# A new beginning for the attention and expert pipeline of one core: TensorE warmed, five places for x, weight halves moved to GpSimd, a shorter routing, gathers behind combinations

## The chip, the cores and the metric

The kernel runs on one core of a Trainium2 chip. The metric is the device time of one execution in microseconds (us). The engines are TensorE (PE, its weight loads PEld), VectorE (DVE), ScalarE (ACT) and GpSimd (POOL); SP, ACT and POOL issue DMAs.

## The reference

x is 8 batches of 512 tokens of 256 channels, in float32. One block is computed:

```python
xn = layernorm(x)
out = x + attn(xn) + ffn(xn)
# attn: latent = xn @ w_kv_down (256->128); k, v = latent @ w_kv_up; q = xn @ w_q
#       16 heads of 64, scores / 8, causal mask, softmax, y @ w_out
# ffn:  scores = sigmoid(xn @ gate_w.T + lb_bias); top 2 of 8 experts, weights normalised
#       for each expert e: wmean = mean weight of the tokens that chose e
#       out += where(chosen, mlp_e(xn) * wmean, 0);  mlp = silu(x gw) * (x uw) @ dw
#       out += shared mlp(xn)
```

The gate's results decide which tokens go to which expert, so they must be exact enough that no choice changes.

## The kernel before, in words

**Halves.** Most products are made from two rounded halves of each float32 operand, H and L = value − H, as three products HH, HL, LH (the helper `three`, lines 673 to 675). ACT copies H (`copy`, line 870), and a subtraction on DVE (`low`, line 1154) or on POOL makes L. Each weight passes through this once, in pieces `split_w` ("d", kA, qA, vA for the first two or four heads, and qB, kB, vB for the rest), `w_out`, and `split_moe` for the ten experts' weights, which are stored to HBM (`wm_scratch`) and loaded again for each block.

**Order.** `work_order` writes one list of ticks by hand. The 128 heads of all batches are taken in pairs P = 0 to 63. A pair lasts four units u, so u = 4P is its start; work with another rhythm is placed by `at(u, ...)`. In a pair: `recip`, `scores` of pair P+1 in three steps, what is placed at 4P, `attend` of pair P−1, `transposes` of the probabilities of the pair's two heads in three steps each, and what is placed at 4P+1 to 4P+3. What is placed before u = 0 is the prologue. Each engine walks the same ticks in order and does its share of a piece some ticks later (`LAG`). An engine never overtakes its own order: it waits at a semaphore with all that comes after.

**Pieces around the change.** `norm_stats` (DVE bn_stats and bn_aggr, then the reciprocal root on POOL), `norm_scale` (DVE, then a store of the normalised x), `norm_rows` (PE transposes to channels on partitions, ACT and DVE make the halves in `wr` or, for batch 0, `xs`), `gate_logits` and `gate_columns`. The seven later batches' transposed x is stored to `xs_scratch` and loaded again 32 units apart. x itself has two places in `acc`, so the load of batch b+2 waits until batch b is transposed and stored. `latent`, `query` and `key` make q and k of a pair (one place for each, `qk`, so their copies wait for the scores of the pair before), `value` makes v of half of four heads, `out_part` multiplies by w_out.

**Routing.** When all logits are there, `route_ops` finds the two experts of each token, counts them (two products by a matrix of ones and a triangle, `totals`), and works out the slot of each token in 39 blocks of 256: 64 DVE operations and four copies, each waiting for the one before. Then `select` and `tokens` (16 steps) invert the slots. From u = 54 the blocks' rows are gathered from `xn_scratch` (`block_load`, POOL), transposed (`block_rows`), multiplied (`gate_up`, `down`) and stored to `y_scratch`.

**The end.** After the last block, for each batch, `rows_load` gathers eight sets of expert rows on POOL, each into the place that a `combine` (DVE) of the batch before has read.

Weights in their raw form stand in buffers that later work uses: raw q in two of the four probability buffers `pp`, raw k in `acc`, raw v in `xr`.

Of the kernel before, what the change touches and what calls it, by code (L numbers as in the profile page):

```python
# [10 lines left out]
ALU = mybir.AluOpType  # L11
# [19 lines left out]
ROUTE_SUMS = 23  # L31
ROUTE_GAP = 12
ROUTE_OPS = 64
# [7 lines left out]
BUSY_HEADS = range(7, 22)  # L41
# [5 lines left out]
AT = {"query": (0.0, 0.9), "key": (2.3, 2.0), "value": (1.1, 2.1), "out_part": (3.2, 0.2), "stats": -3.7,  # L47
      "scale": -2.2, "rows": -1.6, "first": 54.0, "last": 176.0, "split": -1.3, "experts": 23.0, "shared0": 17.0,
# [20 lines left out]
def work_order():  # L69
# [60 lines left out]
    now, loads = 0, [17.5] * 3  # L130
    for start, group in plan:
# [22 lines left out]
        for k in range(k0, k0 + len(group)):  # L154
            loads[k % 3] = max(loads[k % 3], AT["experts"] + 18)
# [79 lines left out]
def attention_moe_kernel(nc, x, w_q, w_kvd, w_kvu, w_out, gate_w, lb_bias, w_moe, consts, out):  # L235
    ctx = ExitStack()
    with ctx:
# [31 lines left out]
        w_raw = sb("w_raw", [128, 2, 768])  # L269
        hh = sb("hh", [128, 3, 2, 512], F32R)  # L270
# [38 lines left out]
        d_xin = [new_sem(f"d_xin{i}") for i in range(2)]  # L309
# [3 lines left out]
        d_xn = [new_sem(f"d_xn{i}") for i in range(2)]  # L313
# [1175 lines left out]
```

## Time and profile before

| | |
|---|---|
| median of three runs | 995.25 us (992.63 to 995.55) |
| the profiled execution | 993.73 us, span 991.9 us |
| instructions | 20064 |
| DMA | 142.76 MB, mean 144 GB/s |
| VectorE, ScalarE, GpSimd busy | 693.2, 666.1, 353.0 us |

A busy share is an average over stages. In a kernel in which one engine does nearly all that can be done in most stages, the places where that engine is idle tell more: the windows give them by stretch, the waits name what ended them, and the timeline shows what stood in between. An instruction's idle time is named with the instruction that released it. The granted clock is TensorE's, as a share of 2.4 GHz.

### The profile page before, as it was taken

The page shows a single profiled execution, that of the slowest core. Times are in us where ns is not written, and L with a number is a line of the kernel's source. Part 1 is how long each engine was busy: PE and PEld are TensorE (multiplying, and loading weights), DVE is VectorE, ACT ScalarE, POOL GpSimd, SP SyncE. Part 2 cuts the span into 40 slices and gives each one's busy share as a digit, 9 for nine tenths or more (in the row PEclk, how much of TensorE's full clock was granted, in tenths as well). Part 3 has the DMA queues.
Part 4 walks back from the last instruction along what each step waited for, and adds up shares of the span by engine and source line. Part 5 has one row for each costly group of instructions (what it writes and reads, how often), then busy time and mean ns, then how long its engine had stood idle before and what let it go on. Part 6 is the DMA issues. An engine that isn't in the chain of part 4 may idle for free.

```text
span 991.9 us, 20064 instructions
## 1 busy us (share of the span) xinstructions
PE 942.5 (95%) x7008; PEld 748.6 (75%) x7008; DVE 693.2 (70%) x2000; ACT 666.1 (67%) x1930; POOL 353.0 (36%) x349
## 2 busy tenths in 40 slices
PE   5589998999999999999999999999999999999998
PEld 4456776678878888888888878888787677777776
DVE  5779599876666576665666666666666677788874
ACT  3756767776776667766677766767667665677662
POOL 0231113653332344333443324343222544444431
PEclk9799999999999999999999999999999999999999
DMA  7387424643326256453554444546434343433321
GB/s 226 125 318 259 163 74 146 207 145 114 110 84 213 69 157 188 143 154 125 159 163 164 151 131 153 163 140 165 149 127 150 93 126 115 150 107 108 107 76 43
DMA packets 66003, 142.76 MB, mean 144 GB/s; under 512 B 7856, under 2 KB 40880, under 8 KB 64112
## 3 DMA queue, kind: packets, MB, share of 16 engines
q1 hardware_dynamic: 52896, 91.77, 28.3%
q0 software_dynamic: 12432, 49.29, 15.8%
q8 instruction: 57, 0.93, 0.4%
q10 hardware_dynamic: 576, 0.42, 0.2%
q14 instruction: 42, 0.34, 0.1%
HBM read 104.76 MB, written 36.70 MB: 143 GB/s over the span
## 4 chain that ended last, share of the span: by engine, by line
PE 72%; DVE 13%; issue 9%; ACT 2%; another core or an unknown queue 2%; POOL 2%; DVEq 0%; POOLq 0%; ACTq 0%
PE PS L673 13%; PE PS L675 12%; PE PS L674 12%; PE PS L721 11%; PE PS L712 11%; PE PS L702 8%; DVE pp L1258 4%; PE PS L696 2%; PE PS L829 2%; DVE acc L1345 1%; DVE pt L1264 1%; DVE yf L1276 1%; DVE qk L1154 1%; DVE acc L1294 1%
## 5 line engine op out<-in xcount | busy, mean ns | idle before, releaser
L938 ACT ACTIVATE pp<-pp,nmax 128x128 f32<-128x128 f32 (+3 forms) x512 | 281.2, 553 | 110.4 <-DVE nmax L1258 76.0
L1258 DVE CUSTOM_DVE_ANT_0 pp<-PS,maskw 128x128 f32<-128x128 f32 (+3 forms) x512 | 216.7, 483 | 32.6 <-remote 23.8
L1419 POOL TENSOR_TENSOR yy<-yf,yy 128x512 fp32r<-128x512 f32 x63 | 81.5, 1293 | 260.2 <-ACT yy L870 259.8
L712 PE MATMUL PS<-ident,pp 128*128 128x128 f32 x1280 | 166.3, 276 | 1.4 <-ACT pt L870 0.6
L721 PE MATMUL PS<-pt,vv 128*64 128x512 f32 (+3 forms) x1024 | 154.5, 439 | 0.5 <-DVE nmax L1258 0.3
L712 PEld LDWEIGHTS PS<-ident,pp 128*128 128x128 f32 x1280 | 140.8, 140 | 17.7 <-issue 10.1
L721 PEld LDWEIGHTS PS<-pt,vv 128*64 128x64 f32 x1024 | 70.1, 136 | 91.4 <-issue 74.8
L702 PE MATMUL PS<-qk 64*128 64x256 f32 (+2 forms) x1152 | 122.2, 349 | 3.6 <-DVE acc L1294 2.2
L870 ACT ACTIVATE pt<-PS 128x384 f32<-128x384 f32 (+1 forms) x215 | 108.5, 512 | 4.1 <-PE PS L712 4.1
L1264 DVE COPY pt<-PS 128x384 f32<-128x384 f32 x169 | 99.2, 591 | 14.1 <-PE PS L712 12.0
L1413 POOL TENSOR_TENSOR hh<-hf,hh 128x256 fp32r<-128x256 f32 (+1 forms) x55 | 49.7, 903 | 138.3 <-ACT hh L870 136.7
L938 ACT ACTIVATION_READ_ACCUMULATOR pp<-pp,nmax 128x1 f32 x512 | 97.4, 190 | 0.0
L702 PEld LDWEIGHTS PS<-qk 64*128 64x128 f32 x1152 | 89.6, 188 | 9.4 <-issue 6.2
L1395 POOL DMA_INDIRECT xr<-xn_scratch,lg x78 | 74.5, 955 | 36.9 <-issue 13.8
L1406 POOL DMA_INDIRECT xg<-y_scratch,lg x64 | 63.3, 990 | 50.5 <-DVE acc L1345 35.4
L673 PE MATMUL PS<-woH,yy 128*128 128x256 f32 x256 | 78.1, 305 | 2.4 <-POOL yy L1419 2.0
L1240 DVE SCALAR_TENSOR_TENSOR qk<-PS,qk 128x512 fp32r<-128x512 f32 x64 | 44.0, 688 | 44.1 <-ACT qk L923 40.5
L674 PE MATMUL PS<-woL,yy 128*128 128x256 f32 x256 | 72.2, 282 | 0.0
L675 PE MATMUL PS<-woH,yy 128*128 128x256 f32 x256 | 72.2, 282 | 0.0
L870 ACT ACTIVATE yy<-yf 128x512 fp32r<-128x512 f32 (+1 forms) x65 | 40.4, 623 | 44.5 <-DVE yf L1276 38.2
L870 ACT ACTIVATE qk<-PS 128x128 f32<-128x128 f32 (+1 forms) x128 | 48.4, 429 | 24.8 <-PE PS L675 20.7
L1154 DVE TENSOR_TENSOR qk<-PS,qk 128x512 fp32r<-128x512 f32 x64 | 44.0, 688 | 28.8 <-ACT qk L870 28.6
(171 smaller groups left out, 2119.9 us busy)
## 6 DMA issues: line engine op xcount, KB each, us to landing
rb<-rr_scratch SPq DMA_DIRECT2D x128, 128.0 KB
wr<-wm_scratch SPq DMA_DIRECT2D x16, 768.0 KB, 5.7
y_scratch<-acc SPq DMA_DIRECT2D x39, 256.0 KB
acc<-in_x SPq DMA_DIRECT2D x15, 512.0 KB, 5.4
wm_scratch<-hh SPq DMA_DIRECT2D x10, 768.0 KB, 4.0
xs_scratch<-wr SPq DMA_DIRECT2D x7, 1024.0 KB, 5.7
xs<-xs_scratch SPq DMA_DIRECT2D x7, 1024.0 KB, 4.8
xn_scratch<-acc SPq DMA_DIRECT2D x8, 512.0 KB, 3.4
```

The lines of the kernel that those rows point to most:

```text
L673: e.matmul(o, aH, bH, start=first and i == 0, stop=False)
L674: e.matmul(o, aH, bL, start=False, stop=False)
L675: done = e.matmul(o, aL, bH, start=False, stop=last and i == len(pairs) - 1)
L702: done = e.matmul(bank(kind, i, 2 * j + h)[:, at:at + n], a[r, q], m[r, 0:n], start=first is True, stop=first is None)
L712: done = e.transpose(o, pp[:, i % 4, P_AT[t] + 128 * kt:P_AT[t] + 128 * kt + 128], ident[:, :])
L721: done = e.matmul(g[64 * h:64 * h + 64, 128 * kt:512], vv[:, i // 2 % 2, kt, n % 4, :], pt[:, h, PT_AT[kt]:PT_AT[kt] + 512 - 128 * kt], st ...
L870: return e.activation(o, i, ACT.Copy)
L938: e.activation(scores, scores, ACT.Exp, scale=-1.0, bias=nmax[:, b, t:t + 1], accum_out=rs[:, i % 4, 2 * t + h:2 * t + h + 1]).then_inc(a_ ...
L1258: e.tensor_tensor_reduce(pp[:, b, P_AT[t]:P_AT[t] + n], g[:, at:at + n], maskw[:, 512 - n:512], -1.0, 3e38, ALU.add, ALU.min, accum_out=nm ...
L1264: e.tensor_copy(pt_part(i, j), bank(kind, i, j)[:, 0:512 if j == 0 else 384]).then_inc(v_pt, 1)
L1395: e.indirect_dma_start(xr[:, 2 * (b % 2) + t, :], None, xn_d[:, :], bass.IndirectOffsetOnAxis(token_of[:, n:n + 1], 0)).then_inc(d_xr[b % ...
L1419: e.tensor_tensor(yy[:, i % 2, 1, :], yf[:, :], f32(yy[:, i % 2, 0, :]), ALU.subtract).then_inc(g_yl, 1)
```

## The change

- PE multiplies a constant by itself 15 times at the start and 5 times ahead of the first latent product (`warm`).
- The first batch's x comes by two queues. x has five places (two in `acc`, three in a new buffer `xp`); batches 1 to 4 are loaded at the start, 5 to 7 into places that come free. Seven batches are normalised 2.35 units apart instead of 2, somewhat later. The transposed x of the last batch goes to `xg`, the block buffer. ACT's queue issues the stores to `xs_scratch`.
- The halves L of qB, kB and vB are made on POOL. Query 1 and key 1 stand elsewhere in the prologue, and query 2 is ahead of scores 1. The mask is loaded as 128 columns, and POOL clears the rest.
- ACT makes all copies of transposed probabilities from head 2 to 21 (before: 7 to 21).
- Four experts are split ahead of the first shared block (before: two, in the prologue), the other six from u = 25.9.
- The routing has 51 operations, 38 of them ahead of the selection and 13 beside it; running sums are made by scan instructions, and the sums of weights by two products with 256 columns.
- At the end the gather for the next batch stands directly behind the combination that frees its place.

```diff
-ROUTE_SUMS = 23
+ROUTE_SUMS = 19
 ROUTE_GAP = 12
...
-BUSY_HEADS = range(7, 22)
+LATE_PARTS = WEIGHT_PARTS[4:]
+BUSY_HEADS = range(2, 22)
+EARLY_SPLITS = 4
...
+AT = {"query": (0.0, 0.9), "key": (2.3, 2.0), "value": (1.1, 2.1), "out_part": (3.2, 0.2), "stats": -1.6,
+      "scale": 0.2, "rows": 1.2, "first": 54.0, "last": 176.0, "experts": 25.9, "shared0": 19.2,
       "shared7": 248.0, "finish": (255.5, 257.2, 258.2), "fix": 8.0, "loading": 2.3, "xs": -9.4, "down": 4.6}
...
+    def norm_at(b):
+        return 2.35 * (b - 2) + 3.0 if b > 1 else 0.0
+
     for P in range(NHT // 2):
-        at(4 * (P - 2) + AT["query"][P % 2] if P else -9, "query", P)
-        at(4 * (P - 2) + AT["key"][P % 2] if P else -8, "key", P)
+        at(4 * (P - 2) + AT["query"][P % 2] if P > 2 else (-9, -6, -1.5)[P], "query", P)
+        at(4 * (P - 2) + AT["key"][P % 2] if P > 1 else (-8, -3.5)[P], "key", P)
     for Gr in range(NHT // 4):
         at(4 * (2 * Gr - 2) + AT["value"][0], "value", Gr, 0)
         at(4 * (2 * Gr - 1) + AT["value"][1], "value", Gr, 1)
...
             at(u + AT["xs"], "xs_load", b)
         at(u - 8.05 if b else -10, "latent", b)
         at(u + 8, "acc_load", b)
...
-        at(2 * b + AT["scale"], "norm_scale", b)
-        at(2 * b + AT["rows"], "norm_rows", b, 0)
-        at(2 * b + AT["rows"] + 0.05, "norm_rows", b, 1)
+        at(norm_at(b) + AT["stats"], "norm_stats", b)
+        at(norm_at(b) + AT["scale"], "norm_scale", b)
+        at(norm_at(b) + AT["rows"], "norm_rows", b, 0)
+        at(norm_at(b) + AT["rows"] + 0.05, "norm_rows", b, 1)
     for b in range(NBATCH):
-        at(2 * b + 0.7, "gate_logits", b)
-        at(2 * b + 1.8, "gate_columns", b)
+        at(norm_at(b) + 2.3 if b else 0.7, "gate_logits", b)
+        at(norm_at(b) + 3.4 if b else 1.8, "gate_columns", b)
     for c in range(2):
         at(4 * c, "w_out", c)
     for i in range(NW):
-        at(2 * i + AT["split"] if i < 2 else 2 * i - 4 + AT["experts"], "split_moe", i)
-    at(18, "routing")
+        at((8.0, 12.0, 15.0, 17.3)[i] if i < 4 else 2 * i - 8 + AT["experts"], "split_moe", i)
+    at(18.6, "routing")
     for i in range(3):
-        at(17.5, "ring_load", i)
...
         at(32 * b + 38, "store", b)
     for r, b in enumerate(FIX_ORDER):
         f = last_block + 8 + AT["fix"] * r
         for n in range(8):
-            at(f + 0.8 * n - (3 if r else 0), "rows_load", r, n)
+            if r == 0:
+                at(f + 0.8 * n, "rows_load", r, n)
             at(f + 3.3 + 0.65 * n, "combine", r, n)
+            if r + 1 < len(FIX_ORDER):
+                at(f + 3.31 + 0.65 * n, "rows_load", r + 1, n)
...
     for c in range(2):
         put("norm_rows", 0, c)
         tick()
+    put("split_w", "qA")
+    put("split_w", "vA")
 
...
         ticks[at_tick + int((k + ROUTE_GAP) * ROUTE_TICKS)].append(("route",))
-    end = at_tick + int((ROUTE_OPS + ROUTE_GAP) * ROUTE_TICKS)
+    end = at_tick + int((ROUTE_MAIN + ROUTE_GAP) * ROUTE_TICKS)
+    for k in range(ROUTE_OPS - ROUTE_MAIN):
+        ticks[end + 4 + 3 * k // 2].append(("route",))
...
+        def xT_flat(b):
+            return wr_flat(b % 2) if b < NBATCH - 1 else xg[:, :, :, :, :].rearrange("p q a c n -> p (q a c n)")
+
+        x_home = {b: (0, 1, 2, 3, 4, 0, 1, 2)[b] for b in range(NBATCH)}
+        x_turn = {b: sum(x_home[a] == x_home[b] for a in range(b + 1)) for b in range(NBATCH)}
+        x_next = {b: next((a for a in range(b + 1, NBATCH) if x_home[a] == x_home[b]), None) for b in range(NBATCH)}
+
         def x_in(b):
-            return acc[:, 1 + b % 2, :, :]
+            return acc[:, 1 + x_home[b], :, :] if x_home[b] < 2 else xp[:, x_home[b] - 2, :, :]
+
+        def x_stored(b):
+            return d_xn[x_home[b]], 16 * x_turn[b]
 
         def xT_part(b, c):
...
                 return xs[:, 0, c, :], xs[:, 1, c, :]
...
+                    e.dma_start(rows128(xn_d[i * T:i * T + T, :]), x_in(i)).then_inc(x_stored(i)[0], 16)
+                elif kind == "norm_rows" and lag == 4 and j and x_next[i]:
                     w.wait_ge(p_xt, 2 * i + 2)
-                    w.wait_ge(d_xn[i % 2], 16 * (i // 2 + 1))
-                    e.dma_start(x_in(i), rows128(x[i + 2])).then_inc(d_xin[i % 2], 16)
-                elif kind == "gate_logits" and lag == 0 and i >= 1:
-                    w.wait_ge(v_xtl, 2 * i + 2)
-                    e.dma_start(xs_d[i], f32(wr_flat(i % 2))).then_inc(d_xsd[i % 2], 16)
+                    w.wait_ge(*x_stored(i))
+                    e.dma_start(x_in(i), rows128(x[x_next[i]])).then_inc(x_loaded(x_next[i], 0)[0], 16)
                 elif kind == "xs_load" and lag == 0:
                     w.wait_ge(d_xsd[i % 2], 16 * ((i + 1) // 2) if i % 2 else 16 * (i // 2))
...
 
+            def warm(n):
+
+                for _ in range(n):
+                    e.matmul(bank("latent", 0, 0)[:, 0:128], ones[:, :], ones[:, :], start=True, stop=True)
+
+            w.wait_ge(g_cst, 1)
+            warm(15)
...
                     w.wait_ge(*xs_ready(b))
-                    w.wait_ge(v_wlo, whi_at["qA" if p < 2 else "qB"])
...
                 elif kind == "latent":
+                    if not i:
+                        warm(5)
...
-                    e.matmul(g2[:, 0:8], ones[:, :], e1[:, :], start=True, stop=True).then_inc(p_tot, 1)
+                    e.matmul(g2[:, 0:256], ones[:, :], rv("s"), start=True, stop=False)
+                    e.matmul(g2[:, 0:256], ones[:, :], rv("w"), start=False, stop=True).then_inc(p_tot, 1)
...
+            for t in range(2, 4):
+                e.dma_start(x_in(0)[:, t, :], x[0, 128 * t:128 * t + 128, :]).then_inc(d_x0[t], 16)
+            e.dma_start(ident[:, :], consts[:, 0:128]).then_inc(d_ident, 16)
             e.dma_start(gw[:, :, :], gate_w).then_inc(d_gw, 16)
-            e.dma_start(hf[:, 0, :], consts[:, 800:1312]).then_inc(d_mask, 16)
-            e.dma_start(lb[:, :], lb_bias).then_inc(d_lb, 16)
-            e.dma_start(kc[:, :], consts[:, 384:672]).then_inc(d_kc, 16)
 
...
                         w.wait_ge(d_wmd[s], 16 * (i // 2))
+                    if i >= EARLY_SPLITS:
...
+                elif kind == "gate_logits" and lag == 1 and i:
+                    w.wait_ge(v_xtl, 2 * i + 2)
+                    e.dma_start(xs_d[i], f32(xT_flat(i))).then_inc(d_xsd[i % 2], 16)
...
-                tt(rv(b_)[:, sh:256], rv(a_)[:, sh:256], rv(a_)[:, 0:256 - sh], ALU.add)
...
+            w.wait_ge(p_tot, 1)
+            w.wait_ge(g_cst, 1)
+            g, g2 = bank("totals", 0, 0), bank("totals", 1, 0)
+            own()
+            e.tensor_tensor_scan(rv("tot"), ones[:, 0:1].to_broadcast([128, 256]), g[:, 0:256], 0.0, ALU.mult,
+                                 ALU.add).then_inc(v_ro, 1)
+            yield
+            tt(rv("pos"), g[:, 256:512], rv("tot"), ALU.add)
+            yield
+            w.wait_ge(p_tot, 2)
+            reduce(wm[:, :], g2[:, 0:256].rearrange("p (t e) -> p e t", e=8), ALU.add)
+            yield
...
+            yield
+
+            cp(slot_of, m12[:, :])
+            yield
+            ts(e1[:, :], n_tok, 1.0, None, ALU.max)
+            yield
+            recip(e1[:, :])
+            yield
+            tt(wm[:, :], wm[:, :], e1[:, :], ALU.mult)
+            yield
+            for k in range(2):
+                tt(rv3("s"), rv3(f"c{k}"), bt(wm[:, :]), ALU.mult)
+                yield
+                reduce(coef[:, 32 * k:32 * k + 32], rv3("s"), ALU.add)
+                yield
...
+            e.memset(maskw[:, 0:384], 0.0).then_inc(g_cst, 1)
...
+                elif kind == "split_w" and lag == 0 and i in LATE_PARTS:
+                    raw, _, oH, oL = raw_w[i]
+                    w.wait_ge(a_whi, whi_at[i])
+                    e.tensor_tensor(oL, raw, f32(oH), ALU.subtract).then_inc(g_wlo, 1)
...
-                    e.tensor_tensor(out_w(i)[2], acc[:, 0, :, :].rearrange("p t n -> p (t n)"), f32(out_w(i)[1]),
-                                    ALU.subtract).then_inc(g_wo, 1)
+                    raw = acc[:, 0, :, :].rearrange("p t n -> p (t n)")
+                    for s in (slice(0, 512), slice(512, 1024)):
+                        done = e.tensor_tensor(out_w(i)[2][:, s], raw[:, s], f32(out_w(i)[1][:, s]), ALU.subtract)
+                    done.then_inc(g_wo, 1)
```

## Rows read from the trace of the kernel before

**Rows 1.** The page: busy time by engine, and PE's tenths in 40 slices.

```profile
PE 942.5 (95%) x7008; PEld 748.6 (75%) x7008; DVE 693.2 (70%) x2000; ACT 666.1 (67%) x1930; POOL 353.0 (36%) x349
...
PE   5589998999999999999999999999999999999998
```

**Rows 2.** Windows: busy of PE, PEld, DVE, ACT, POOL, then clock, DMA share, GB/s.

```profile
0.00:22.00 22.00, 10.42 (x51) 7.67 (x51) 9.99 (x31) 7.41 (x16) 1.85 (x8) 1.00 0.79 253
22.00:40.00 18.00, 7.66 (x42) 6.25 (x41) 14.80 (x43) 11.14 (x31) 3.32 (x3) 0.72 0.15 52
40.00:110.00 70.00, 63.16 (x436) 44.41 (x437) 54.26 (x176) 45.84 (x124) 17.93 (x18) 0.98 0.73 257
110.00:200.00 90.00, 82.56 (x608) 62.93 (x606) 79.20 (x228) 65.57 (x188) 32.21 (x26) 0.98 0.43 146
200.00:800.00 600.00, 596.43 (x4547) 486.17 (x4544) 390.52 (x1119) 415.37 (x1209) 225.42 (x228) 1.00 0.45 143
800.00:992.00 192.00, 182.23 (x1338) 141.14 (x1337) 144.40 (x406) 120.80 (x367) 72.25 (x67) 1.00 0.32 100
```

**Rows 3.** Waits of PE, 0 to 200 us: total, times, longest.

```profile
PE PS L696 <- DVE qk L1240: 13.8, 4, 10.3
PE PS L793 <- DVE acc L1175: 8.7, 1, 8.7
...
PE PS L673 <- DVE xs L1154: 1.4, 1, 1.4
PE PS L673 <- DVE wvL L1154: 1.2, 1, 1.2
```

**Rows 4.** Timeline, 0 to 40 us: start, length, instruction, idle before.

```profile
5.81 0.43 DVE L1164 BATCH_NORM_STATS2 st<-acc 128x6 f32<-128x256 f32 x1 [0.26 <-DMA acc<-in_x]
...
8.71 2.21 PE L793 MATMUL PS<-ident,acc 128*128 128x128 f32 x8 [8.71 <-DVE acc L1175]
...
12.92 0.63 PE L674 MATMUL PS<-xs,wdH 128*128 128x512 f32 x1
...
16.25 0.40 PE L674 MATMUL PS<-xs,wqH 128*128 128x512 f32 x1
...
20.32 1.82 PE L702 MATMUL PS<-qk 64*128 64x256 f32 x17
...
27.17 0.59 ACT L923 ACTIVATE qk<-PS 128x512 fp32r<-128x512 f32 x1
...
28.12 1.50 ACT L870 ACTIVATE wqH<-pp 128x1536 fp32r<-128x1536 f32 x1
...
29.65 1.76 DVE L1154 TENSOR_TENSOR wqL<-pp,wqH 128x1536 fp32r<-128x1536 f32 x1 [2.81 <-ACT wqH L870]
...
31.33 0.95 DVE L1154 TENSOR_TENSOR wkL<-acc,wkH 128x768 fp32r<-128x768 f32 x1
31.89 2.05 POOL L1371 TENSOR_TENSOR hh<-w_raw,hh 128x768 fp32r<-128x768 f32 x1 [3.60 <-ACT hh L870]
32.20 2.55 DVE L1154 TENSOR_TENSOR wvL<-xr,wvH 128x768 fp32r<-128x768 f32 x1
34.67 0.68 DVE L1240 SCALAR_TENSOR_TENSOR qk<-PS,qk 128x512 fp32r<-128x512 f32 x1
...
35.88 3.26 PE L702 MATMUL PS<-qk 64*128 64x256 f32 x18
```

**Rows 5.** Windows of 2 us, columns as in rows 2.

```profile
78.00:80.00 2.00, 2.00 (x9) 1.25 (x8) 2.00 (x8) 2.00 (x9) 0.00 (x0) 0.50 0.61 141
...
174.00:176.00 2.00, 2.00 (x6) 1.43 (x5) 2.00 (x8) 0.27 (x2) 0.88 (x2) 0.50 0.62 243
```

**Rows 6.** DVE's waits, 40 to 110 us; then the issues of one line.

```profile
DVE st L1164 <- DMA acc<-in_x: 3.8, 2, 3.0
```
```profile
L573 SPq DMA_DIRECT2D xs_scratch<-wr x7: 332/681/1753, 51.3 to 101.2; - x7
```

**Rows 7.** Waits of the whole run, POOL's for combinations.

```profile
POOL xg L1406 <- DVE acc L1345: 35.4, 13, 5.0
```

More of the change, by code:

```diff
@@ L129, in work_order @@
     plan.sort(key=lambda x: x[0])
-    now, loads = 0, [17.5] * 3
+    now, loads = 0, [17.0] * 3
     for start, group in plan:
@@ L308, in attention_moe_kernel @@
         d_x0 = [new_sem(f"d_x0{i}") for i in range(4)]
-        d_xin = [new_sem(f"d_xin{i}") for i in range(2)]
+        d_xin = [new_sem(f"d_xin{i}") for i in range(5)]
         d_ident, d_mask, d_gw, d_lb, d_kc = (new_sem("d_" + n) for n in ("ident", "mask", "gw", "lb", "kc"))
@@ L312, in attention_moe_kernel @@
         d_wout = new_sem("d_wout")
-        d_xn = [new_sem(f"d_xn{i}") for i in range(2)]
+        d_xn = [new_sem(f"d_xn{i}") for i in range(5)]
         d_xsd = [new_sem(f"d_xsd{i}") for i in range(2)]
@@ L373, in attention_moe_kernel, with low_weights @@
         whi_at = {n: i + 1 for i, n in enumerate(WEIGHT_PARTS)}
+        def low_weights(name):
+            return (g_wlo, whi_at[name] - 4) if name in LATE_PARTS else (v_wlo, whi_at[name])
         group_of = {k: item[-1] for k, item in enumerate(items)}
@@ L542, in hh_free @@
                 return ((p_dn, down_done(k - 3)),)
-            return tuple((sem, 16 if k < 2 else 16 * (NW // 2)) for sem in d_wmd)
+            return tuple((sem, 8 * EARLY_SPLITS if k < 2 else 16 * (NW // 2)) for sem in d_wmd)
         def f32(a):
@@ L549, in sync_program @@
             w = Waits(e)
-            for t in range(4):
+            for t in range(2):
                 e.dma_start(x_in(0)[:, t, :], x[0, 128 * t:128 * t + 128, :]).then_inc(d_x0[t], 16)
-            e.dma_start(ident[:, :], consts[:, 0:128]).then_inc(d_ident, 16)
             for name in WEIGHT_PARTS:
@@ L555, in sync_program @@
                 if name == "vA":
-                    e.dma_start(x_in(1), rows128(x[1])).then_inc(d_xin[1], 16)
+                    e.dma_start(hf[:, 0, 0:128], consts[:, 1184:1312]).then_inc(d_mask, 16)
+            for b in range(1, 5):
+                e.dma_start(x_in(b), rows128(x[b])).then_inc(x_loaded(b, 0)[0], 16)
+            e.dma_start(lb[:, :], lb_bias).then_inc(d_lb, 16)
+            e.dma_start(kc[:, :], consts[:, 384:672]).then_inc(d_kc, 16)
             def moe_load(q):
@@ L583, in sync_program @@
                     w.wait_ge(p_xt, 2 * NBATCH)
-                    for b in (NBATCH - 2, NBATCH - 1):
-                        w.wait_ge(d_xn[b % 2], 16 * (b // 2 + 1))
+                    for b in range(NBATCH - 3, NBATCH):
+                        w.wait_ge(*x_stored(b))
                     e.dma_start(rv("tri", 128), consts[:, 672:800]).then_inc(d_tri, 16)
@@ L900, in scalar_program @@
                     w.wait_ge(p_xt, 2 * NBATCH)
-                    for b in (NBATCH - 2, NBATCH - 1):
-                        w.wait_ge(d_xn[b % 2], 16 * (b // 2 + 1))
+                    for b in range(NBATCH - 3, NBATCH):
+                        w.wait_ge(*x_stored(b))
                     e.activation(rv("s"), lgf, ACT.Exp, scale=-1.0).then_inc(a_sig, 1)
@@ L1031, in route_ops @@
             w.wait_ge(p_xt, 2 * NBATCH)
-            for b in (NBATCH - 2, NBATCH - 1):
-                w.wait_ge(d_xn[b % 2], 16 * (b // 2 + 1))
+            for b in range(NBATCH - 3, NBATCH):
+                w.wait_ge(*x_stored(b))
             ts(rv("s"), rv("s"), 1.0, None, ALU.add)
```

147 lines of the change are left out of this document (60 added, 87 removed).

## The prediction

> **What bounds the kernel now.** The page comes first: TensorE (PE) is busy for 942.5 of 991.9 us, and its tenths are low only at the start [rows 1]. The windows then put the idle time in its place. From 200 to 800 us PE is idle 3.6 of 600 us: there the time is PE's own work, which the change leaves as it is, and every microsecond gained earlier is carried to the end one for one. Idle elsewhere: 11.6 us in 0 to 22, 10.3 in 22 to 40, 6.8 in 40 to 110, 7.4 in 110 to 200, 9.8 after 800 [rows 2]. So the most that a new beginning can give is some 36 us of idle and what the slow clock costs beside it. The waits name what ends the gaps: before 200 us nearly all are DVE's, one of 10.3 us, and 8.7 us are the wait for the first normalised x [rows 3].
>
> The 10.3 us gap can be read in the timeline. ACT is busy with exponentials until it copies key 1 at 27.17; then it rounds the late weights (28.12 on), DVE subtracts three of them in order (wqL, wkL, wvL, 29.65 to 34.75), and the low half of key 1 stands behind them and begins at 34.67. Scores 1 start at 35.4 [rows 4]. PE then comes back at about half pace: the 18 score matmuls take 3.26 us, where 17 took 1.82 before [rows 4]. In 78 to 80 and 174 to 176, each some us after a gap, the granted clock is 0.50, the level of 1.2 GHz [rows 5].
>
> The sum is made on the profiled execution: 993.73 us, with a span of 991.9 and 1.8 outside it. The median of the runs shown is 995.25, 1.5 above it.
>
> **To scores 0 (0 to 22 us).** Two of the four first x tiles move to ACT's queue, so the last is issued two slots of some 0.45 us sooner; bn_stats on it starts at 5.81 now [rows 4]. I take 1.1 us off the wait of 8.7. The 15 warming products run in that wait. The trace has no such product; the nearest row is the 8 transposes of 128 columns in 2.21 us, 0.28 each, so one instruction each gives 4.1 us and two each 8.3, begun at about 0.95: they end between 5.1 and 9.2, and x is due at about 7.6. Cost 0 to 1.6; I take 0, since the transposes of the row themselves wait for DVE. The gain is the clock: matmuls of 512 columns start 0.43 us apart from 12.33 to 15.5 and 0.23 apart after that (0.63 and 0.40 long [rows 4]); 7 at 0.2 are 1.4 us. The five further products stand in the 1.4 us wait for xs [rows 3] and are hidden. Splitting vA sooner removes a wait of 1.2 us, and query 1 now fills PE while key 0 is evicted. Idle goes from 11.6 to about 8.8: 2.8 + 1.4 = **4.2**, with scores 0 at about 17 in place of 20.1.
>
> **The late weights (22 to 40 us).** qB, kB and vB are subtracted on POOL. On DVE they took 1.76 + 0.95 + 2.55 = 5.3 us; POOL takes 2.05 us for 768 columns [rows 4], so 4.1 + 2.05 + 2.05 = 8.2 us. qB comes early: ACT rounds it right behind value 0 (1.50 us, to about 18), POOL is done at about 22. Query 2 needs it and is ahead of scores 1 in PE's order; its 1.4 us end at 23.4. Scores 1 need key 1: before, the copy was there 7.7 us after scores 0 had begun at 20.1, and its low half, 0.7 long, would have been at 8.4; the copy now comes after four exponentials instead of eight, so 6.5 to 8.4, that is 23.5 to 25.4. PE has about 5 us of work in between, which leaves a gap of 1.5 to 3.4; I take 2.8. What is late next is value (1,0), which needs vB. ACT copies query 2 only after scores 1, so it rounds kB and vB at about 26.3 to 27.8, and POOL is done 4.1 us later, about 31; PE gets there at about 28. I take 2.8 us (0 if vB's rounding slips ahead, 5 if POOL is held). Idle 10.3 becomes 5.6: 4.7, and the half clock behind it goes, 1.4 on the scores and 0.5 on their neighbours: **6.6**.
>
> POOL's row and DVE's give a ratio of 2.05 to 0.95, and wvL, which ran beside POOL's subtraction (31.89 to 33.94), took 2.55 us for the same 768 columns [rows 4]. The Trainium skill has both: GPSIMD Engine Reference, Engine selection, sends elementwise work with two inputs to VectorE, as GpSimd is about half as fast; SBUF — State Buffer, Who interferes with whom, says that a DVE instruction with two SBUF inputs and a GpSimd instruction that reads SBUF exclude each other for the whole instruction. The trace agrees with both. By these rules the move loses 3 us of engine time and could block DVE besides; what stands on DVE meanwhile are mostly reads of PSUM, which by the same section don't collide.
>
> **x in five places, norms further apart (40 to 110 us).** Now DVE waits 3.8 us for x [rows 6], and in this stretch it is busy 54.3 of 70 us in bursts [rows 2]. With four batches loaded at the start these waits go. The norms come every 2.35 units instead of 2, and all probability copies from head 2 on are ACT's. Per pair of heads that is, as an estimate from the durations in the timeline, about 13.7 us of DVE, 14 of ACT and 15.4 of PE, against 16.5 of DVE and 16.2 of PE before: PE becomes the bound, but narrowly. Idle 6.8 to 3.0: 3.8. Half clock at 77 to 80 gone: 1.3. **5.1**. The stores of xs move to ACT's queue. SP needs 0.33 to 1.75 us for an issue, median 0.68 [rows 6]: seven cost ACT 2.3 to 12.3 us, over 4.5 pairs. At the median that is 1.1 us per pair, just hidden; at the top ACT leads PE by some 1.5 us per pair, 7 us in all. Whether v_xtl is waited for costs nothing: ACT's copy of the logits ahead of it already stands behind it.
>
> **Routing (110 to 200 us).** DVE is busy 79.2 of 90 us [rows 2]. 64 operations and 4 copies become 51; 38 are ahead of the selection, 13 beside it. Some 17 fewer at 0.2 to 0.45 us are 5 to 6 us less of DVE. Of 7.4 us idle I leave 4.0, since the 13 now fall into the selection: 3.4. The slow clock at 171 to 176 [rows 5]: 1.4. The weight sums become two products of 256 columns instead of one of 8: 0.85 more PE. **3.95**. Four early expert splits move 1.8 us units of POOL and 0.8 of ACT forward into idle time.
>
> **The end.** Each gather stands right behind the combination that frees its place. POOL waits 35.4 us for those combinations now, to nobody's harm [rows 7]. 0 to 2 us, I take 0.5.
>
> Sum: 4.2 + 6.6 + 5.1 + 3.95 + 0.5 = 20.35; 0.6 is given back for a half clock after the two new gaps. 993.73 − 19.7 = **974.0 us**.
>
> **Rivals.** (A) As above, 974; its own range is 967 to 983. (B) The head is freed more fully: no gap for vB, no idle after 40 us. Then 4.2 + 11.2 + 8.1 + 8 + 2 = 33.5, and 960 to 967. For it speaks that PE reaches 10.0 of 10 wherever DVE isn't late; against it the narrow margins of 1.5 us per pair. (C) ACT or DVE becomes the bound in the first 20 units: the issues on ACT at 1.75 us (7 us lost), vB at 5 us, and routing's 13 late operations cost what they save (3.4): 974 + 7 + 2.2 + 3.4 = 986.6; 983 to 992. (D) On the other side, one mechanism at the end: POOL now stands at a gather until DVE has done the combination just ahead of it, and the low half of yy, which out_part waits for, stands behind on POOL. About 9 out_part groups lie in those 72 units. The slack is some 2 us; DVE is busy 144 of 192 us there [rows 2], and POOL's longest wait for a combination is 5.0 us [rows 7]. If each group costs more than 2.2 us, the 19.7 are gone; at 5.0 − 2.0 = 3.0 it is 27, so 1001. Against it: the wait exists already without PE waiting for POOL there. (E) The beginning gains but the gaps only move, within 0.3% (3 us, about what separates a real difference from none here): 992 to 997.
>
> **Numbers.** A 0.60, B 0.14, C 0.18, E 0.03, D 0.05. 966 to 987 keeps A nearly whole and the larger part of C, and leaves out about 2 in 10. Faster by over 0.3%: A, B and C, 0.92; same 0.03; slower 0.05.
>
> **What would show it.** Right: matmuls of the first latent 0.23 us apart; scores 0 near 17, scores 1 near 24, no PE gap over 4 us after 10 us; the idle sum before 200 us at 20 to 23 instead of 36.2; 200 to 800 unchanged. Wrong: a PE gap before query 2 or value (1,0) above 5 us (POOL too slow), xs stores of over 1 us on ACT with PE waiting for ACT between 40 and 90, new waits for POOL's yy after 760, or PE busy per window in the middle that differs.

## The result, and the profile after

The changed kernel takes 1013.06 us (median of 4 runs, 1011.01 to 1014.83); the kernel before, run beside it, takes 993.94 (4 runs, 991.66 to 995.55). The ratio is 1.0189, with a 95% interval of 1.0170 to 1.0208: slower by 1.9%, where 974.0 us and a range of 966 to 987 had been forecast. Case D, given 0.05 and 1001 us, is what happened, and it cost more than it was priced at. The profiled run took 1014.83 us, with a span of 1013.0. Of the executions of the experiments below, one of E6 (5102.92 us) and one of the kernel before (1530.11) were in a slow state, and the ratios leave them out.

The page after, as in [rows 1], with the tenths of the granted clock:

```profile
PE 955.4 (94%) x7050; PEld 762.3 (75%) x7050; DVE 675.2 (67%) x1973; ACT 670.7 (66%) x1937; POOL 361.5 (36%) x355
...
PE   8699998999999999999999999999997998888988
...
PEclk9999999999999999999999999999999898899999
```

PE's tenths fall towards the end, where [rows 1] has only nines up to the last, and the clock dips there too. The windows, columns as in [rows 2]:

```profile
0.00:22.00 22.00, 18.77 (x106) 15.31 (x106) 10.21 (x32) 9.62 (x19) 5.62 (x10) 1.00 0.82 258
22.00:40.00 18.00, 12.15 (x83) 8.34 (x82) 14.29 (x55) 15.85 (x48) 5.68 (x6) 1.00 0.34 107
40.00:110.00 70.00, 63.30 (x433) 44.76 (x432) 51.06 (x166) 50.38 (x138) 22.51 (x22) 0.95 0.74 260
110.00:200.00 90.00, 84.43 (x642) 64.80 (x641) 78.23 (x233) 63.85 (x183) 40.14 (x36) 1.00 0.50 169
200.00:800.00 600.00, 590.63 (x4487) 483.37 (x4487) 383.87 (x1095) 413.62 (x1202) 215.32 (x217) 0.99 0.44 138
800.00:1013.00 213.00, 186.15 (x1307) 145.68 (x1306) 137.51 (x394) 117.40 (x353) 72.22 (x67) 0.94 0.29 88
```

Against [rows 2], idle in 22 to 40 us falls from 10.3 to 5.9 and in 110 to 200 from 7.4 to 5.6; in 40 to 110 it stays (6.8 and 6.7) and the clock is lower (0.98 and 0.95). From 200 to 800 it goes from 3.6 to 9.4, and after 800 us from 9.8 to 26.9. The waits name the cause; first PE's, then POOL's, of the whole run (total, times, longest):

```profile
PE PS L700 <- POOL yy L1463: 29.5, 8, 7.0
```
```profile
POOL xg L1450 <- DVE acc L1382: 68.7, 24, 4.6
```

PE's wait for POOL's low half of yy, 2.0 us in 3 waits in the kernel before, is now PE's largest. Six of its 8 waits are long: 6.99 us at 786.55 (inside the window 200 to 800), and five of 4.25 to 4.35 after that. POOL's wait for combinations has doubled from 35.4 us in 13 to 68.7 in 24 [rows 7]. One such place, first on POOL and then on PE:

```profile
839.30 1.14 POOL L1450 DMA_INDIRECT xg<-y_scratch,lg  x1 [3.87 <-DVE acc L1382]
...
844.70 0.95 POOL L1450 DMA_INDIRECT xg<-y_scratch,lg  x1 [0.30 <-issue]
845.66 1.27 POOL L1463 TENSOR_TENSOR yy<-yf,yy 128x512 fp32r<-128x512 f32 x1
```
```profile
846.99 0.58 PE L700 MATMUL PS<-woH,yy 128*128 128x256 f32 x1 [4.35 <-POOL yy L1463]
847.37 0.41 PE L701 MATMUL PS<-woL,yy 128*128 128x256 f32 x1
```

POOL stands 3.87 us at the first gather until DVE has combined. Then five gathers take some 1.25 us of POOL each (mostly 0.95 and a gap of 0.30), and only then comes the low half of yy. ACT had finished its high half at 840.88 (840.25, 0.63 long), so it lies ready for 4.8 us. PE waits 4.35 us for it and comes back at half pace: 0.41 us for 256 columns, and a granted clock of 0.50 over 847 to 851:

```profile
847.00:851.00 4.00, 4.00 (x22) 3.78 (x24) 0.94 (x2) 0.00 (x0) 0.00 (x0) 0.50 0.05 13
```

The kernel before has the same wait at its corresponding place, also 3.87 us long, but one gather and not five between it and the low half, which then waits 0.53 us for ACT's high half; its other five gathers follow from 847.06 on:

```profile
843.97 1.14 POOL L1406 DMA_INDIRECT xg<-y_scratch,lg  x1 [3.87 <-DVE acc L1345]
845.63 1.28 POOL L1419 TENSOR_TENSOR yy<-yf,yy 128x512 fp32r<-128x512 f32 x1 [0.53 <-ACT yy L870]
```

The starts of the scores give the account. Ahead of the kernel before by 2.8 us at scores 0 (17.30), 10.5 at scores 1 (24.93), 10.8 in the middle (scores 18 at 291.22 for 302.03), and 10.6 when the combinations begin; behind it by 21.1 at the last scores (979.41 for 958.33). So the beginning gave some 10.8 us (10.6 by the time the combinations begin) and the end took 31.7.

### The profile page after: what moved, and what is told of

The parts are those of the page before. It is cut to its first block, busy times and chain, and to the rows that moved or that the text cites. A ratio compares the mean times of both kernels' runs of the same rounds, so it can differ in the third digit from the quotient of the medians.

```text
span 1013.0 us, 20144 instructions
## 1 busy us (share of the span) xinstructions
PE 955.4 (94%) x7050; PEld 762.3 (75%) x7050; DVE 675.2 (67%) x1973; ACT 670.7 (66%) x1937; POOL 361.5 (36%) x355
## 3 DMA queue, kind: packets, MB, share of 16 engines
q1 hardware_dynamic: 51888, 84.32, 25.9%
## 4 chain that ended last, share of the span: by engine, by line
PE 77%; DVE 9%; POOL 5%; issue 4%; ACT 3%; DMA 1%; another core or an unknown queue 0%; SPq 0%; ACTq 0%; DVEq 0%; POOLq 0%
PE PS L700 14%; PE PS L702 13%; PE PS L701 13%; PE PS L755 12%; PE PS L746 11%; PE PS L736 9%; POOL xg L1450 3%; DVE pp L1295 3%; PE PS L730 2%; PE PS L866 2%; POOL yy L1463 1%; DMA w_raw<-in_w_moe 1%; DVE pt L1301 1%; PE PS L761 1%; ACT pt L907 1%
## 5 line engine op out<-in xcount | busy, mean ns | idle before, releaser
L755 PE MATMUL PS<-pt,vv 128*64 128x512 f32 (+3 forms) x1024 | 152.1, 439 | 0.0
L755 PEld LDWEIGHTS PS<-pt,vv 128*64 128x64 f32 x1024 | 68.0, 137 | 89.9 <-issue 74.2
L907 ACT ACTIVATE pt<-PS 128x384 f32<-128x384 f32 (+1 forms) x222 | 112.3, 513 | 4.0 <-PE PS L746 4.0
L700 PE MATMUL PS<-woH,yy 128*128 128x256 f32 x256 | 81.8, 319 | 29.5 <-POOL yy L1463 29.5
L1301 DVE COPY pt<-PS 128x384 f32<-128x384 f32 x162 | 95.3, 592 | 17.0 <-PE PS L746 12.9
L736 PEld LDWEIGHTS PS<-qk 64*128 64x128 f32 x1152 | 92.1, 194 | 7.7 <-issue 2.1
L1450 POOL DMA_INDIRECT xg<-y_scratch,lg x64 | 64.5, 1009 | 81.4 <-DVE acc L1382 68.7
L700 PEld LDWEIGHTS PS<-woH,yy 128*128 128x128 f32 x256 | 51.8, 202 | 42.0 <-POOL yy L1463 31.4
L1331 DVE TENSOR_TENSOR acc<-acc,PS 128x512 f32<-128x512 f32 x62 | 42.4, 684 | 53.0 <-PE PS L702 46.1
L702 PE MATMUL PS<-woH,yy 128*128 128x256 f32 x256 | 75.7, 296 | 0.0
L701 PE MATMUL PS<-woL,yy 128*128 128x256 f32 x256 | 75.7, 296 | 0.0
```

Of the source, the lines that this page charges most:

```text
L700: e.matmul(o, aH, bH, start=first and i == 0, stop=False)
L701: e.matmul(o, aH, bL, start=False, stop=False)
L702: done = e.matmul(o, aL, bH, start=False, stop=last and i == len(pairs) - 1)
L736: done = e.matmul(bank(kind, i, 2 * j + h)[:, at:at + n], a[r, q], m[r, 0:n], start=first is True, stop=first is None)
L755: done = e.matmul(g[64 * h:64 * h + 64, 128 * kt:512], vv[:, i // 2 % 2, kt, n % 4, :], pt[:, h, PT_AT[kt]:PT_AT[kt] + 512 - 128 * kt], st ...
L907: return e.activation(o, i, ACT.Copy)
```

## Experiments

Each ratio is to the kernel before on the same chip. Four chips were used. The kernel before took 992.2 us on the chip of E1 to E4, 978.9 on that of E5, E6, E10 and E11, 979.4 on that of E7 to E9 and E12, and 992.3 on that of E13 and E15; hence times of different sets are compared by ratio.

### The gathers: E1, E2

E1 is the new kernel with the old line for the gathers, E2 the old kernel with the new one. The edit of E1; E2's is its reverse:

```diff
-            if r == 0:
-                at(f + 0.8 * n, "rows_load", r, n)
+            at(f + 0.8 * n - (3 if r else 0), "rows_load", r, n)
             at(f + 3.3 + 0.65 * n, "combine", r, n)
-            if r + 1 < len(FIX_ORDER):
-                at(f + 3.31 + 0.65 * n, "rows_load", r + 1, n)
```

> The changed kernel with one edit taken back: the gathers stand 1.7 to 2.75 units behind the combinations they wait for, as before the change. Theory H (held queue: POOL stands at a gather until DVE has combined, and the low half of yy behind it comes late for out_part): the 7 gaps of 4.3 to 7 us at out_part and the half clock behind each go, which together cost 31.7 us from scores 45 to scores 63 (from 10.6 ahead of the kernel before to 21.1 behind it); time 981 to 984. Rival S (the new beginning shifts all later work, so that the end collides in any case): time stays above 1000, gaps at out_part remain.

E1: 981.21 us (980.35 to 983.80), ratio 0.9892 (0.9866 to 0.9917). PE's waits for yy are 0.9 us in all. Its span of 979.4 is 33.6 under that of the changed kernel. PE is idle 23.6 us less (34.0 for 57.6) and busy 10.0 less (945.4 for 955.4) with the same 7050 instructions. So a good part of the loss isn't in the gaps themselves: after the long gaps PE runs at half clock, and that is counted as busy. POOL still waits 34.7 us for combinations here, and that costs nothing.

> The kernel before with only the new places of the gathers. Theory H: the loss does not need the new beginning, so 994 + 31.7 = about 1025, with gaps of 4 to 7 us at out_part. Rival S: under 1000, no such gaps.

E2: 1024.09 us (1022.50 to 1025.88), ratio 1.0324 (1.0301 to 1.0347), 31.9 us slower. The wait is the same as in the changed kernel:

```profile
PE PS L676 <- POOL yy L1422: 30.7, 9, 7.0
```

So this one edit costs some 32 us in either kernel, and the rest of the change gives 10.7 (E1: 981.21 for 992.18).

### Waiting, or the place in the queue: E3, E10, E11

E3 and E10 gather alternate batches into `xp`, free by then, so that a gather waits for the combination of two batches earlier; E3 keeps the new order of the gathers, E10 the old. E11 is the changed kernel with its gathers one unit later. Of E3 the changed wait is shown; the lines that name the second buffer and its semaphores are left out:

```diff
-                    if i:
-                        w.wait_ge(v_fx, 8 * (i - 1) + j + 1)
+                    if i > 1:
+                        w.wait_ge(v_fx, 8 * (i - 2) + j + 1)
+                    elif i:
+                        w.wait_ge(p_xt, 2 * NBATCH)
```
```diff
-                at(f + 3.31 + 0.65 * n, "rows_load", r + 1, n)
+                at(f + 4.31 + 0.65 * n, "rows_load", r + 1, n)
```

> The changed kernel, with its gathers where the change puts them, but every second batch gathers into the free x buffer, so that a gather waits for the combination of two batches earlier, long done. Theory H, by the wait: POOL issues the gathers when it gets to them, the gaps go, 981 to 985. Rival B (burst: the gathers' own 1.25 us each, five to seven of them ahead of the low half of yy, are the cost, wherever they stand in this order): 1005 to 1015, since as many gathers stand ahead of yy as now.

E3: 1007.81 us (1007.46 to 1009.21), ratio 1.0158 (1.0136 to 1.0180). POOL's waits for combinations are down to 0.3 us and PE's for yy to 1.5, yet only 0.3% comes back. So seven gathers ahead of the low half don't make it late when none of them has had to wait. But now POOL issues seven gathers without a pause, DVE stops meanwhile, and PE waits for DVE by name. On POOL, on DVE and on PE:

```profile
826.95 0.97 POOL L1453 DMA_INDIRECT xp<-y_scratch,lg  x1 [0.15 <-issue]
...
834.47 0.94 POOL L1453 DMA_INDIRECT xp<-y_scratch,lg  x1 [0.30 <-issue]
```
```profile
836.46 0.69 DVE L1351 TENSOR_TENSOR acc<-acc,PS 128x512 f32<-128x512 f32 x1 [5.91 <-remote]
```
```profile
838.34 0.79 PE L701 MATMUL PS<-xs,wqH 128*128 128x512 f32 x1 [5.59 <-DVE pt L1302]
```

DVE's addition at 836.46 waits for a product that the trace shows ended at 830.75, and starts 1.04 us after the last gather's end at 835.41. SP's next load, of expert weights into `wr`, is released at 836.45 too.

> The changed kernel with the second place for gathered rows and the gathers in their old places in the order. Nothing then holds POOL at a gather, and no more than the old number of gathers stands ahead of the low half of yy. Theory Q (only the place in the queue counts): 979 to 983, as the run with the gathers as before. Theory R (gathers that nothing holds run off in one burst of seven or eight, and other engines' waits end late during it, as in the second-place run, where DVE, SP and ACT stood 5.7 to 5.9 us until the burst was over): 990 to 1008, with waits put down to a remote or unknown releaser.

E10: 968.75 us (968.43 to 969.58), ratio 0.9890 (0.9863 to 0.9918), as E1. Its gathers come in runs of three and five, most of them directly behind a low half, and PE doesn't stop:

```profile
827.71 1.28 POOL L1463 TENSOR_TENSOR yy<-yf,yy 128x512 fp32r<-128x512 f32 x1 [8.37 <-ACT yy L905]
829.14 0.97 POOL L1450 DMA_INDIRECT xp<-y_scratch,lg  x1 [0.15 <-issue]
...
834.16 0.95 POOL L1450 DMA_INDIRECT xp<-y_scratch,lg  x1 [0.30 <-issue]
```

> The changed kernel with each gather one unit further behind its combination (1.01 instead of 0.01 units; before the change 1.7 to 2.75). If the loss comes from gathers that stand ahead of the low half of yy by their place in the order, part of them now stand behind it: 985 to 1003, with gaps at out_part of 1 to 3 us. If the nearness to the combination alone counts, so that one unit of distance is enough: 980 to 984.

E11: 980.39 us (978.97 to 983.83), ratio 1.0011 (0.9993 to 1.0029), 11.6 us over E10. The wait for a combination is the same 3.87 us at the place that corresponds, but three gathers stand between it and the low half in place of five. The first row is from the waits, then POOL's timeline and PE's:

```profile
PE PS L700 <- POOL yy L1463: 11.5, 7, 1.9
```
```profile
828.67 1.14 POOL L1450 DMA_INDIRECT xg<-y_scratch,lg  x1 [3.87 <-DVE acc L1382]
...
832.54 1.27 POOL L1463 TENSOR_TENSOR yy<-yf,yy 128x512 fp32r<-128x512 f32 x1
```
```profile
833.86 0.39 PE L700 MATMUL PS<-woH,yy 128*128 128x256 f32 x1 [1.86 <-POOL yy L1463]
834.09 0.28 PE L701 MATMUL PS<-woL,yy 128*128 128x256 f32 x1
```

The 11.5 us of waits are nearly the whole difference to E10, for after 1.86 us PE's products still take 0.28. Two gathers fewer make PE's wait 2.49 us shorter (1.86 for 4.35), which is two issues of 1.25. Four fewer than five, as in the kernel before, would by the same step leave nothing, and PE has no such wait there. So the lateness of the low half is made of two parts: the first gather is held, and the gathers behind it in the same order are issued after it. Without the hold (E3) PE hardly waits for yy (ACT is late there too by the stops, but in E10 two such low halves are 12.0 us apart, 852.71 and 864.70, and seven gathers need 8.7), and with the hold but one gather (the kernel before, E1) it doesn't either. A second place is worth nothing in the old order (E10 as E1).

### A long unbroken run of gathers: E13

E13 is E10 with all eight gathers of a batch in one place.

```diff
-            at(f + 0.8 * n - (3 if r else 0), "rows_load", r, n)
+            at(f + (0.8 * n if r == 0 else 0.01 * n), "rows_load", r, n)
```

> The kernel with a second place for the gathered rows and the old order of the gathers (ratio 0.989 so far, in bursts of three and five gathers), but the eight gathers of a batch stand in one place, at the middle of where they stood. No gather waits for a combination in either. Theory U (a long unbroken run of gathers on POOL holds up other engines, as the 5.91 and 5.73 us stops with releaser remote in the kernel with the second place and the new order): stops of 3 to 6 us in most of the seven rounds, 15 to 35 us slower than the old order, ratio 1.005 to 1.025, and PE not waiting for POOL's yy in them. Theory V (only a low half that stands behind gathers matters): the burst stands directly behind a low half as before, so no stop, ratio 0.988 to 0.992; if a low half of yy lies behind it, PE waits for POOL's yy by name.

E13: 1008.36 us (1006.90 to 1008.93), ratio 1.0153 (1.0133 to 1.0172), with 0.6 us of PE's waits for yy in all. Theory U holds by time and by place: the stops come with the runs of gathers, though only one of DVE's waits named remote is above 5 us, and the others are up to 4.5. On the same chip E15, with the old order and the second place, has ratio 0.9918, so the loss isn't the chip's. POOL, DVE, PE and ACT around one run:

```profile
806.13 0.97 POOL L1450 DMA_INDIRECT xg<-y_scratch,lg  x1 [0.15 <-issue]
...
814.92 0.95 POOL L1450 DMA_INDIRECT xg<-y_scratch,lg  x1 [0.30 <-issue]
```
```profile
815.69 0.69 DVE L1329 TENSOR_TENSOR acc<-acc,PS 128x512 f32<-128x512 f32 x1 [5.69 <-remote]
```
```profile
816.52 1.65 PE L734 MATMUL PS<-qk 64*128 64x512 f32 x6 [3.44 <-issue]
```
```profile
817.86 0.60 ACT L1014 ACTIVATE hf<-PS 128x512 f32<-128x512 f32 x1 [8.29 <-remote]
```

### The beginning, part by part: E4 to E9, E12, E15

E4 to E9 are E1 with one thing undone. E4 makes the low halves of qB, kB and vB on DVE again. E5 has no warming products. E6 makes the low halves of w_out on DVE. E7 has all 51 routing operations ahead of the selection. E8 shares the copies of heads 2 to 6 again. E9 has the norms 2 units apart. E15 is E10 with the edits of E6 and E9. E12 is the kernel before with the new order of the prologue alone. Cuts of the edits of E5, E8, E9 and E12:

```diff
-            warm(15)
...
-                        warm(5)
```
```diff
-BUSY_HEADS = range(2, 22)
+BUSY_HEADS = range(7, 22)
```
```diff
-        return 2.35 * (b - 2) + 3.0 if b > 1 else 0.0
+        return 2.0 * b if b > 1 else 0.0
```
```diff
-        at(4 * (P - 2) + AT["query"][P % 2] if P else -9, "query", P)
-        at(4 * (P - 2) + AT["key"][P % 2] if P else -8, "key", P)
+        at(4 * (P - 2) + AT["query"][P % 2] if P > 2 else (-9, -6, -1.5)[P], "query", P)
+        at(4 * (P - 2) + AT["key"][P % 2] if P > 1 else (-8, -3.5)[P], "key", P)
...
-    for u, name in ((-8.5, "vA"), (-1.3, "qB"), (-1.2, "kB"), (-1.1, "vB")):
+    for u, name in ((-6.5, "qB"), (-1.2, "kB"), (-1.1, "vB")):
...
-    put("split_w", "qA")
...
+    put("split_w", "qA")
+    put("split_w", "vA")
```

The head of E1 is that of the changed kernel, yet its scores 2 start at 42.14 and not at 40.43, and its scores 4 at 80.27 and not at 80.87. So starts in the head, read from one trace each, differ by up to 2 us for no cause in the code.

> As the first of these runs (gathers as before the change), and qB, kB and vB are subtracted on DVE again, at their new places in the order. If the move to POOL gave the head's gain: 4 to 8 us above the first run, with a gap before scores 1 as in the kernel before. Rival (the new order gave it, since key 1 now stands ahead of kB and vB): within 1.5 us of the first run, or faster, as DVE needs 5.3 us for what POOL needs 7.1.

E4: 983.33 us (982.12 to 984.65), ratio 0.9911 (0.9890 to 0.9933), 2.1 us over E1 with intervals that overlap, and between the two expectations. The move to POOL is worth some 2 us, if anything.

> Gathers as before the change, and the 20 warming products left out. By the prediction they give 1.4 us, by 512-column matmuls 0.23 instead of 0.43 us apart in the first latent and query: 1.4 to 2.5 us above the run with the gathers as before, that is 982.5 to 983.7. Rival (the first work is bound by ACT and DVE behind PE): within 0.7 us of it.

E5: 968.97 us (966.89 to 970.22), ratio 0.9893 (0.9870 to 0.9916), as E1. Without warming the first products of 512 columns last 0.63 to 0.79 us and scores 0 start at 18.76 (E1: 17.41), but scores 4 at 80.22 (80.27).

> Gathers as before the change, and the low halves of w_out made on DVE instead of POOL. Between 40 and 61 us four tensor_scalar instructions of norm_scale took 3.31, 2.35 and 2.43 us instead of 1.37 while POOL subtracted w_out, and PE had gaps of 1.48 and 1.45 us and half clock behind them. If that collision is what kept idle time at 6 us in 40 to 110 where 3.0 was predicted: 3 to 5 us faster, 976 to 978. Rival (DVE's own 2.4 us for the two subtractions take it back): 980 to 983.

E6: 969.10 us (967.71 to 971.91 without the one of 5102.92), ratio 0.9899 (0.9872 to 0.9925). Scores 4 come at 79.50, and the time is that of E1.

> The kernel before with one part of the change: the order of the prologue (halves qA and vA behind the first x, query 1 and key 1 earlier, half qB earlier, query 2 ahead of scores 1). Everything else, the split of late weights on DVE and the gathers too, is as before. Theory H (this order gives the whole gain that the new kernel keeps when its gathers stand as before, 1.1% or some 10.7 us): 7 to 11 us faster, ratio 0.989 to 0.993, scores 1 near 26 us in place of 35.4. Theory S (the gain is a sum of many parts, as predicted: 4.7 of it from the order and the move to POOL together): 3 to 5 us faster, ratio 0.995 to 0.997.

E12: 976.42 us (973.12 to 978.16), ratio 0.9965 (0.9952 to 0.9979). Scores 1 start at 27.56, 7.9 us ahead of before, as theory H had it; but at scores 2 only 2.1 are left, and the time is as theory S had it. What is late next stands in PE's timeline:

```profile
27.56 0.49 PE L697 MATMUL PS<-qk 64*128 64x128 f32 x4 [1.07 <-DVE qk L1241]
35.07 2.21 PE L794 MATMUL PS<-ident,acc 128*128 128x128 f32 x8 [5.44 <-DVE acc L1176]
```

The transposes of batch 1's x wait 5.44 us for its norm. The order alone doesn't keep its gain; with the rest of the change it does (E1). Which part of the rest keeps it wasn't tried: the early loads and the new places of the norms are likely by this row, and the spacing of 2.35 isn't needed (E9).

> The new kernel with its gathers as before and the norms 2 units apart again in place of 2.35. Theory S (spacing is worth what was predicted, 3.8 of idle and 1.3 of clock, less the part that the loads give): 2 to 4 us slower than with 2.35, ratio to before 0.992 to 0.994. Theory H: within 1 us, ratio 0.988 to 0.990.

E9: 966.45 us (964.40 to 968.23), ratio 0.9872 (0.9858 to 0.9887), the lowest ratio measured, and 2 and 3.6 us under E8 and E7 of the same set, which neither theory had said. The wider spacing doesn't help. In the changed kernel the scaling of x meets subtractions on POOL: at 40.51 that for w_out, at 53.58 a low half of yy (54.40, 1.37 long). DVE's rows, then POOL's first:

```profile
40.51 3.31 DVE L1220 TENSOR_SCALAR xp<-xp,mv,rstd 128x256 f32<-128x256 f32 x4 [0.20 <-POOL rstd L1401]
...
53.58 2.35 DVE L1220 TENSOR_SCALAR xp<-xp,mv,rstd 128x256 f32<-128x256 f32 x4
```
```profile
40.72 2.64 POOL L1410 TENSOR_TENSOR woL<-acc,woH 128x512 fp32r<-128x512 f32 x2 [0.24 <-ACT woH L907]
```

In E9, where POOL does nothing at those times, four such instructions take

```profile
44.06 1.38 DVE L1217 TENSOR_SCALAR xp<-xp,mv,rstd 128x256 f32<-128x256 f32 x4
...
51.85 1.37 DVE L1217 TENSOR_SCALAR xp<-xp,mv,rstd 128x256 f32<-128x256 f32 x4
```

> The new kernel with its gathers as before, but copies of transposed probabilities of heads 2 to 6 shared between DVE and ACT again. Theory S (DVE was the bound in 40 to 110 us and ACT took its load): 1 to 3 us slower than with range 2 to 22, ratio 0.991 to 0.993. Theory H: within 1 us, ratio 0.988 to 0.990.

E8: 968.41 us (967.22 to 969.51), ratio 0.9886 (0.9871 to 0.9900): the copies are worth nothing that shows.

> The new kernel with its gathers as before, but all 51 routing operations ahead of the selection. Theory S (the 13 moved operations load the 12 us of the selection, and 38 ahead of it leave PE 3.4 us less idle): moving them back gives 1 to 3 us away, ratio 0.991 to 0.993. Theory H: within 1 us either way, ratio 0.988 to 0.990.

E7: 970.09 us (969.03 to 972.23), ratio 0.9912 (0.9898 to 0.9925). The 13 late operations beside the selection may be worth about 2 us, as theory S said, but the interval overlaps that of E1.

> The new kernel with the old order of the gathers, the second place for gathered rows, the norms 2 units apart, and the low halves of w_out on DVE. If the two small gains add up (ratios 0.9872 and 0.9899 beside 0.989 for the kernel without either): ratio 0.985 to 0.988, 12 to 15 us under the kernel before. If they have the same source (DVE and POOL meeting in 40 to 62 us): 0.987 as with the spacing alone.

E15: 985.69 us (983.24 to 986.58), ratio 0.9918 (0.9896 to 0.9939). A miss for both expectations: the two edits don't add up, and together they are no better than E1. Its scores 2 start at 43.72 (E9: 39.90) after a wait of 1.90 us for DVE's `qk`. DVE's timeline says what stood ahead of that:

```profile
41.84 1.23 DVE L1197 TENSOR_TENSOR woL<-acc,woH 128x1024 fp32r<-128x1024 f32 x1 [2.69 <-ACT woH L905]
42.98 0.68 DVE L1277 SCALAR_TENSOR_TENSOR qk<-PS,qk 128x512 fp32r<-128x512 f32 x1
```

DVE is held 2.69 us at the subtraction for w_out until ACT has its high half, and the low half of `qk` comes behind it at 42.98; in E9 it comes at 38.53. In E6 the same pair stands at 40.40 and 41.54, and scores 2 wait 2.05 us. It is the mistake of the gathers once more, on another engine. At scores 4 E15 is 4.7 us behind E9 (81.50 for 76.77), and its ratio is 4.5 us worse; so this fits, with one trace of each. It ran on another chip than E9, and E9's lead over E1, 2 us with intervals that overlap, stays a likely gain and no more.

## Why the prediction was wrong

**The step that failed is "The end": "0 to 2 us, I take 0.5".** It read POOL's 35.4 us of waits [rows 7] as harmless, which they were, because at most one gather stood between a held gather and the low half of yy. It didn't put the new order of POOL's queue beside the old, and counted no gathers. The term is −31.7 us by the scores' starts, and −31.9 by E2. The runs show in its place a gather held for 3.0 to 4.5 us with four more of some 1.25 us behind it (five times; the first time one held for 1.74 us with six behind it). That made six waits of PE of 4.25 to 6.99 us, with half clock after them.

**Rival D named the mechanism and priced half of it; that its 27 us are near the 29.5 measured is luck.** It took the longest wait for a combination, 5.0, less 2.0 of slack, for 9 groups. The wait alone does nothing: with one gather behind it the kernel before had the same 3.87 us and no wait of PE at that place. What was left out is the issue time of the gathers that are held with it, 1.25 us each. The measured waits are six and not nine, of 4.8 us in the mean and not 3.0. The half clock behind the gaps was left out too: E1 has 10.0 us less of PE's busy time. An argument against D ("without PE waiting for POOL there") held for the old order alone, and there not quite (2.0 us in 3 waits). The prediction named the sign itself, new waits for POOL's yy after 760. 0.05 was too little for a risk with a worked price of 27 us.

**To scores 0 and the late weights: right in the sum.** 4.2 + 6.6 = 10.8 was forecast, 10.5 was there at scores 1: scores 0 at 17.30 for "about 17", scores 1 at 24.93 for 23.5 to 25.4, idle in 22 to 40 at 5.9 for 5.6. By part it was 2.8 and 7.7, so the first is too large and the second too small. The first adds 1.4 us of clock to 2.8 of idle, though it moves scores 0 by 3.1 only (20.1 to 17). PE's timeline in the head:

```profile
0.98 6.05 PE L708 MATMUL PS<-ones 128*128 128x128 f32 x30 [0.98 <-POOL half L1389]
24.93 0.49 PE L730 MATMUL PS<-qk 64*128 64x128 f32 x4 [1.06 <-DVE qk L1276]
...
32.37 0.39 PE L700 MATMUL PS<-wvH,lat 128*128 128x256 f32 x1 [0.87 <-POOL wvL L1405]
```

The warming products took 6.05 us, between the bounds of 4.1 and 8.3: two records each, as the upper bound had it, but of 0.20 us. Value (1,0) waited 0.87 us in place of 2.8, since POOL's three subtractions took 7.1 us (3.48 + 1.84 + 1.81) where 8.2 were put. Two parts were given too much: warming brings scores 0 forward by 1.4 us, as said, but nothing to the end (E5), and POOL instead of DVE is some 2 us, if anything (E4). One sign of being right was met by this alone: the idle before 200 us came to 21.4 for the 20 to 23 forecast, but the warming products, 6.05 + 1.28 us that move nothing, count as busy in it.

**x in five places (5.1) and routing (3.95): next to nothing shows of them.** From scores 1 to scores 18 the lead grows from 10.5 to 10.8, where 8.5 more were forecast (9.05 less the 0.6 given back). In 40 to 110 us idle is 6.7 for the 3.0 forecast, and the clock falls where it was to rise. The sum seems to have added terms of which one is the condition of another: in E12, without the other edits, 5.8 of the 7.9 us won at scores 1 are gone at scores 2, and PE waits for a norm of x. So the edits to x probably earn their keep in the 6.6, not in 5.1 of their own; the early loads weren't undone by themselves, so this is argued and not shown. And the sum let DVE's scaling lie beside POOL at no cost; it takes up to 3.31 us there where 1.37 are enough. The Trainium skill, SBUF — State Buffer, Who interferes with whom, counts tensor_scalar among the operations that may take the port pair shared with GpSimd; the trace agrees, with 3.31 and 2.35 us beside POOL's work and 1.38 and 1.37 apart from it (E9). What it costs isn't shown: E6 takes the subtraction for w_out off POOL and is no faster, having put it ahead of other work on DVE. The prediction used that section for the subtractions and left this half of it out. Routing came to 5.6 us of idle for 4.0; perhaps 2 us of its gain are real (E7). Stores of xs on ACT's queue took 0.33 us each, the low bound, so rival C's price for them was absent.

## What to carry to other kernels

Before moving DMA issues in an in-order queue, write the old and the new order of that queue side by side and ask of each work instruction how many issues, and whose waits, now stand ahead of it; a hold and the issues behind it add up, and here neither did harm without the other. A wait of an engine that is harmless today is so only for what stands behind it today. The same count is due when work is moved to another engine: a subtraction that waits holds all that comes after it (E15). Gains of one stage that may share a condition shouldn't be summed as if each stood alone; a worked price of 27 us deserves more than one chance in twenty.

## What the runs showed of the hardware

- With an unbroken run of seven (E3) or eight gathers (E13) from POOL, DVE stops though none of its waits there is for POOL: it is released 5.9 and 5.7 us after its last work, 1.0 us after the last gather's end and 0.2 before it. The loss against the kernel with shorter runs on the same chip is 26.6 us in E3 (against E1) and 22.7 in E13 (against E15, which has two more edits). With runs of three to five PE keeps working (E10). E1 and the kernel before, with runs of five, have waits of DVE named remote too, up to 2.8 and 3.2 us, yet in E1 PE is busy 227.0 of the 239 us from 740 on; the traces from the chips of E10 and of E9 have none of that name at all. That the longer run is the cause is likely by E13 against E10, which differ in the gathers' places alone; by what path (the engines' signals, the DMA queues) is open, and wasn't tried.
- After PE's gap of 4.35 us the granted clock is 0.50 in 847 to 851 and 256 columns take 0.41 us; after E11's gap of 1.86 us they still take 0.28.
- The same kernel before took 992.2 us on one chip and 978.9 on another, 1.3% apart and more than most of the parts above are worth.
